# P by V in blocks of four key tiles instead of two, with eight P buffers instead of four

## What is computed

```python
x = x + tanh(g_xattn) * attention(layernorm(x), ctx, ctx, mask, ...)   # 16 batches, 56 queries, 1500 keys, 16 heads of 8
x = x + tanh(g_ffn) * ffn(layernorm(x), ...)                           # 8 experts, top 2, and a shared one
```

```python
q, k, v = query @ qw.T + qb, key @ kw.T + kb, value @ vw.T + vb
scores = einsum('bhqd,bhkd->bhqk', q * DH ** -0.5, k)      # masked to -1e9 where mask == 0
probs = softmax(scores)
out = einsum('bhqk,bhkd->bhqd', probs, v) @ ow.T + ob
```

## Time and profile before

| | |
|---|---|
| time, median of 3 runs | 538.66 us (537.0 to 539.79) |
| the profiled execution | 538.73 us, its span 536.9 us |
| PE busy | 477.6 us, 89% |
| DVE / ACT / POOL busy | 399.8 / 328.4 / 218.7 us |
| 82.20 to 381.30 us (units 1 to 13) | PE busy 296.22 of 299.10 us, DVE 240.87, ACT 200.19, granted clock 1.00, DMA share 0.80 |
| 381.30 to 405.60 us (unit 14) | PE busy 22.26 of 24.30 us |
| 405.60 to 421.30 us (unit 15) | PE busy 14.55 of 15.70 us, ACT 12.27 |
| the spread L307 in step 8 of one unit | starts 285.00, next matmul 285.38 |
| two tiles in unit 15, starts | L363 x16 409.92, L382 x32 410.81, L363 x16 411.71 |

### The profile page before, as it was taken

How to read it: one execution, slowest core, us unless ns; L and a number is a source line. 1 busy time by engine, 2 the same in 40 slices (tenths; PEclk the granted TensorE clock), 3 DMA queues, 4 the chain that set the end, 5 groups by cost and what they waited for, 6 DMA issues and landing times.

```text
span 536.9 us, 15752 instructions
## 1 busy us (share of the span) xinstructions
PE 477.6 (89%) x6779; PEld 355.0 (66%) x6779; DVE 399.8 (74%) x749; ACT 328.4 (61%) x414; POOL 218.7 (41%) x184
## 2 busy tenths in 40 slices
PE   0447699999999999999999999999899867999993
PEld 0114376777768677787777768677688645777772
DVE  6339578787788778888787788778776778766656
ACT  2311367667666666767667666766657737787871
POOL 4034326062351615426062351614645899940000
PEclk9859799999999999999999999999999977999997
DMA  5899976996968869697797968858002121100001
GB/s 161 178 231 199 246 186 143 246 196 172 195 159 189 178 164 190 172 207 138 168 198 173 193 158 190 171 102 188 5 3 80 42 77 43 40 1 2 2 1 35
DMA packets 39806, 72.83 MB, mean 136 GB/s; under 512 B 4638, under 2 KB 26271, under 8 KB 39736
## 3 DMA queue, kind: packets, MB, share of 16 engines
q1 hardware_dynamic: 38456, 70.90, 59.1%
q10 hardware_dynamic: 1280, 0.92, 0.7%
HBM read 24.28 MB, written 0.46 MB: 46 GB/s over the span
## 4 chain that ended last, share of the span: by engine, by line
PE 76%; DVE 8%; DMA 5%; ACT 4%; issue 3%; SPq 2%; POOL 1%; ACTq 0%; DVEq 0%
PE ring L342 16%; PE pv L382 16%; PE st L363 11%; PE ring L324 8%; PE st L828 7%; PE ring L286 7%; PE ring L881 6%; DMA ctxT<-in_ctx 4%; DVE max_part L536 2%; SPq L268 2%; DMA ident_h<-in_c_ident_h 2%; ACT v_ext L469 2%; PE pv L881 2%; PE ring L307 1%; PE ring L350 1%
## 5 line engine op out<-in xcount | busy, mean ns | idle before, releaser
L536 DVE TENSOR_REDUCE max_part<-ring 112x1 f32<-112x512 f32 (+1 forms) x384 | 244.8, 675 | 73.1 <-PE ring L342 73.1
L489 ACT ACTIVATE probs<-st 128x896 f32<-128x896 f32 x192 | 172.6, 916 | 73.5 <-PE st L363 71.3
L342 PE MATMUL ring<-keys,qrs 121*112 121x512 f16 (+1 forms) x384 | 149.6, 391 | 6.8 <-DVE max_part L536 3.2
L363 PEld LDWEIGHTS st<-qrs,keys 121*128 121x128 f16 (+1 forms) x1536 | 97.2, 102 | 29.5 <-issue 8.9
L363 PE MATMUL st<-qrs,keys 121*128 121x112 f16 (+1 forms) x1536 | 106.8, 213 | 1.0 <-ACT qrs L478 1.0
L382 PE MATMUL pv<-probs,v_ext 128*32 128x168 f32 (+3 forms) x3072 | 93.6, 262 | 0.1
L382 PEld LDWEIGHTS pv<-probs,v_ext 128*32 128x32 f32 (+1 forms) x3072 | 73.2, 109 | 21.6 <-issue 11.3
L614 POOL TENSOR_TENSOR k_hi<-k_raw,zero 128x512 f16<-128x512 f32 (+1 forms) x45 | 45.9, 1020 | 86.7 <-ACT k_raw L457 86.7
L342 PEld LDWEIGHTS ring<-keys,qrs 121*112 121x112 f16 x384 | 49.9, 130 | 41.6 <-DVE max_part L536 17.5
L856 DVE TENSOR_TENSOR keys<-probs,keys 128x896 f16<-128x896 f32 (+2 forms) x40 | 45.7, 1144 | 26.1 <-ACT keys L849 26.0
L286 PE MATMUL ring<-ctxT,w_qkv 128*128 128x512 f32 (+1 forms) x94 | 52.9, 649 | 12.9 <-DMA ctxT<-in_ctx 12.9
(11 more groups left out here) (116 smaller groups left out, 404.7 us busy)
## 6 DMA issues: line engine op xcount, KB each, us to landing
ctxT<-in_ctx SPq DMA_DIRECT2D x16, 750.0 KB, 6.4
keys<-mask_add SPq DMA_DIRECT2D x32, 375.0 KB
keys<-k_hi SPq DMA_DIRECT2D x32, 375.0 KB, 6.5
keys<-k_lo SPq DMA_DIRECT2D x32, 375.0 KB, 7.7
keys<-mask_add SPq DMA_DIRECT2D x32, 281.2 KB
mask_raw<-in_mask SPq DMA_DIRECT2D x15, 375.0 KB, 3.6
up_w<-in_up_w SPq DMA_DIRECT2D x9, 256.0 KB, 2.7
down_w<-in_down_w SPq DMA_DIRECT2D x9, 256.0 KB, 3.2
```

The source lines that it names most:

```text
L342: nc.tensor.matmul(ring[0:QW, m % 2, 0:width(c)], qrs[0:ROWS, w, p, :, :].rearrange("r h q -> r (h q)"), keys[0:ROWS, w, p, chunk(c)], sta ...
L363: mm = nc.tensor.matmul(st[0:m, j % 2, p // 4, QW * (p % 4):QW * (p % 4 + 1)], keys[0:ROWS, u, p, j * P:j * P + m], qrs[0:ROWS, u, p, :, : ...
L489: nc.scalar.activation(probs[0:m, j % 4, :].rearrange("p (h c) -> p h c", h=2), st[0:m, j % 2, :, 0:HQ // 2], ACT.Exp).then_inc(s["exps_do ...
L536: nc.vector.tensor_reduce(max_part[:, p, c:c + 1], ring[0:QW, m % 2, 0:width(c)], AX.X, ALU.max).then_inc(s["max_read"], 1)
```

## The change

`probs` gets eight buffers (`PB`), and tile j of unit k uses `slot(k, j)`. P by V is issued for four tiles at a time: tiles 8 to 11 of the batch before in step 3, 0 to 3 in step 7, 4 to 7 in step 11, so three blocks of 64 matmuls in a unit; four tiles instead of two remain behind the last unit. The matmuls are the same. `S_ORDER` places the 24 scores anew (24 places as before; (2,4), (3,3), (5,1) and (7,1) are new, (4,3), (5,4), (8,3) and (9,4) gone), and the normalisation moves from step 1 to step 3. The exp's wait for P by V follows the number of buffers.

```diff
+PB = 8
+QUAD = 4
...
-        probs = sb("probs", [P, 4, HQ])
+        probs = sb("probs", [P, PB, HQ])
...
+        def slot(k, j):
+
+            return (KT * k + j) % PB
...
-        S_ORDER = ((0, 0), (0, 1), (1, 0), (1, 1), (1, 4), (2, 0), (2, 1), (3, 1), (3, 4), (4, 1), (4, 2), (4, 3),
-                   (5, 2), (5, 3), (5, 4), (6, 1), (6, 2), (6, 3), (7, 4), (8, 1), (8, 3), (9, 1), (9, 4), (10, 1))
+        S_ORDER = ((0, 0), (0, 1), (1, 0), (1, 1), (1, 4), (2, 0), (2, 1), (2, 4), (3, 1), (3, 3), (3, 4), (4, 1), (4, 2),
+                   (5, 1), (5, 2), (5, 3), (6, 1), (6, 2), (6, 3), (7, 1), (7, 4), (8, 1), (9, 1), (10, 1))
...
-        NORM_STEP, RECIP_STEP = 1, 8
+        NORM_STEP, RECIP_STEP = 3, 8
...
-                                      probs[0:m, j % 4, S * h:S * (h + n)],
+                                      probs[0:m, slot(k, j), S * h:S * (h + n)],
...
-        LAG = 2
-
-        def pe_pv_pair(pe, b, j):
-
-            k, u, t = b
-            if j % 2 and j > LAG and has(k, 0):
-                for i in (j - LAG - 1, j - LAG):
+        LAG = QUAD
+
+        def pe_pv_quad(pe, b, j):
+
+            k, u, t = b
+            if j % QUAD < QUAD - 1:
+                return
+            if j == QUAD - 1 and has(k, -1):
+                for i in range(KT - QUAD, KT):
+                    pe_pv(pe, (k - 1, buf(b, -1), None), i)
+            if j > QUAD and has(k, 0):
+                for i in range(j - 2 * QUAD + 1, j - QUAD + 1):
                     pe_pv(pe, b, i)
-            if j == LAG - 1 and has(k, -1):
-                for i in range(KT - LAG, KT):
-                    pe_pv(pe, (k - 1, buf(b, -1), None), i)
...
-            if j >= 4 or not known(k, 1):
-                act.wait_ge(s["pv_done"], KT * k + j - 3)
-            nc.scalar.activation(probs[0:m, j % 4, :].rearrange("p (h c) -> p h c", h=2),
+            if KT * k + j >= PB:
+                act.wait_ge(s["pv_done"], KT * k + j - PB + 1)
+            nc.scalar.activation(probs[0:m, slot(k, j), :].rearrange("p (h c) -> p h c", h=2),
```

More of the change, by code:

```diff
@@ L444, in pe_unit @@
                 pe_slot(pe, b, j, 3)
-                pe_pv_pair(pe, b, j)
+                pe_pv_quad(pe, b, j)
                 pe_slot(pe, b, j, 4)
```

## The result

The changed kernel takes 547.45 us (median of 4 runs, 547.16 to 548.49), the kernel before 539.22 beside it; the ratio is 1.016 with a 95% interval of 1.0122 to 1.0198. The forecast was 548.2. The profiled execution took 547.43 us, its span 545.6.

A forecast was written before the change was run, and what follows sets the result against it. TensorE, with the largest busy time, was taken as the bound, DMA not. 13 steady units x 0.53 = 6.9, +0.1 (unit 0), +0.4 (unit 14), +2.05 (unit 15) made +9.5 on 538.73: 548.2 us, range 541.5 to 553.

The forecast's parts named there:

- The price of a block: TensorE entering and leaving one P by V block costs 0.26 us beyond its matmuls; three fewer a unit save 0.79.
- A block of 64 in 1.68: Four-tile P by V block on TensorE: 24 ns a matmul plus 0.13 us, the low end; the high end was 2.01.
- Bank waits: In steps 1 to 3, scores wait for a max to free one of two ring banks: 0.33, 0.33 and 0.30 us.
- (5,1): Score in step 5 waits 0.14 us for its bank behind the normalisation, half as long as the old wait.
- V copies: In steps 5 and 6 the second and third V chunks wait for ScalarE's copies, 0.30 us in all.
- group 11: Last transposed score group of a unit waits 0.37 us on TensorE for exp 9 on ScalarE.
- +0.53 a unit: Each of 13 steady units grows by 0.53 us: waits of 1.96 in place of 0.65, less 0.79 for blocks.
- two real waits: In the old unit, a score behind the normalisation and the second V chunk behind ScalarE's copy wait, together 0.65 us.
- The end passed on whole: The last unit's last block comes 2.05 us later and delays everything to the end by as much; bounds 0.5 and 3.5.
- Rival 1: Faster: scores of steps 1 to 3 do not wait for their bank; unit -0.55 us, total 534; chance 0.08.
- Rival 2: No change: bank waits come, ScalarE's exp and V copy waits do not; unit -0.17 us, total 539; chance 0.07.
- Rival 3: Slower still: long blocks run at the pace of the last 64 matmuls; total 554 to 561 us; chance 0.06.

The follow-up runs named there:

- e6_split_blocks: The changed kernel with one score put into the middle of two of its three P by V blocks a unit; 556.1 us (one run).
- the blocks of three: The changed kernel with P by V blocks of three tiles, scores placed anew, normalisation in step 2, pairs in the last unit; 543.2 us, ratio 1.0089.
- the pairs placed anew: The kernel before, with its blocks of two tiles and four P buffers, and only the score places changed; 533.16 us, ratio 0.9901.
- the fours placed anew: The changed kernel with its blocks of four, score places of its own, normalisation in step 6, pairs in the last unit; 538.84 us, ratio 1.0013.
- e2_old_places: The changed kernel with the score places of the kernel before, normalisation still in step 3; 555.6 us (one run).
- e4_half_exp: The changed kernel with the exp of half of the columns left out, those columns set to one at the start; 544.9 us (one run).

## Why the prediction was right, step by step

- **The price of a block, 0.26:** right in the main; one more switch in the changed kernel costs 0.23 to 0.25 (`e6_split_blocks`).
- **A block of 64 in 1.68:** 1.68. The lower bound was the one to take.
- **Bank waits of 0.33 at (1,4) and (2,4), 0.30 at (3,3):** 0.33, 0.33 and 0.31; and that the loss hangs on them was shown by halving the max. The nearest row, unit 0 of the kernel before, was the same event.
- **(5,1) 0.14, V copies 0.30 in all, group 11 0.37:** measured 0.17, 0.28 and 0.38. The second K chunk and the any row, prices that the layout did not question, happened to have room in this order; in the blocks of three they had none.
- **+0.53 a unit:** +0.53 (23.53 against 23.00). The reading that two real waits stand in the old unit missed a third: score (0,0) starts 1.16 behind the first K chunk, where the next group starts 0.86 behind the second (266.81 to 267.97, 268.81 to 269.67) (ScalarE's copy of the turned maxima, which (0,0) waits for, runs from 266.91 to 267.82). It is as long after the change (246.29 to 247.46), so it drops out of the difference.
- **Unit 0 +0.1, unit 14 +0.4, unit 15 +2.05:** unit 0 can't be told, as all that lies ahead of unit 1 came out -1.1 in one profile and +0.07 in the other; the others +0.44 and +2.08.
- **The end passed on whole:** the size is not settled. Between the up matmul and the end another 0.5 came on top in the profiles of the changed kernel, less than that stretch differs by between kernels with the same work in it, and of 1.3 given back in unit 15 some 0.7 were lost again.
- **The sum, +9.5, 548.2:** +8.7 between the two profiles and +8.2 between the medians (547.45 and 539.22). The units and their waits are right by mechanism; that the total stands within 1 us of the forecast is in part luck, since the early start of that profile (-1.1) and the longer end (+0.5) were not foreseen, and the median of the kernel before was 0.56 higher beside the changed one than the 538.66 that the sum started from.
- **Rival 1 (no bank waits):** its unit was put at -0.55, 22.45; with the max halved it was 22.73, since V copies and the exp then wait in their place (two waits behind one). **Rival 2 (ScalarE's waits do not come):** they came, 0.38 at group 11 and 0.28 at the V chunks. **Rival 3 (slow long block):** 1.68 rules it out.

The two pages of the Trainium skill that were held against the layout both bear on the case. TensorEngine Tiling, Key Properties, says that a change of tiling mode drains TensorE. The trace agrees in that going into a block and out of it costs 0.26 us; that this is a drain, and not another cost of the 128x32 matmuls, no run separates. The step from fp16 to fp32 alone does not cost it: a score ahead of an fp32 V half takes its usual 0.22 (256.44 to 256.66). Perfetto Trace Analysis, Identifying Performance Opportunities, says that a gap that repeats on the engine that should be full can mean too little buffer space. In the steady units of the changed kernel three gaps of 0.31 to 0.33 repeat, each released by a max that had to free one of two banks; the earlier trace rows, which the prediction gives for it, shows such a gap once. In this case a new order shortened the unit from 23.00 to 22.53 with the same two banks.

## What to carry to other kernels

A block that is in the way of one engine may be the cover of another. Before fusing blocks, list what stood between two users of the same two-buffer resource, and see whether something as long as the reader's cycle (here 0.61 us a max) still stands there. When an order is written by hand, lay out one period with start-to-start prices from the trace, all waits included: it told the sign and the size here, and its two large misses (threes) were waits that had been left off the list, not wrong prices.

## What the runs showed of the hardware that was not expected

TensorE now and then stops without a releaser that the profile knows ("issue"). The marked stops in the matmuls of units 0 to 13 last 0.31 to 1.77 us: three in the threes, two in the pairs placed anew, four in the fours placed anew, two in `e2_old_places`, one in `e4_half_exp`, none in the profiles of the other kernels. Ten of the twelve stand inside a block of P by V, two in the turn of the maxima; in the threes all three come 9 or 10 matmuls ahead of the end of the third block of the unit. The kernel before shows one long unit of 23.16 among 13; the version in threes has three (1.1, 2.2 and 0.9 us too long), the pairs placed anew two (0.9 and 0.75), the fours placed anew three (0.6, 1.5 and 0.5). In the stretch 262.5 to 266.5 of the threes, around the longest stop, the instruction queue moved one packet, and other transfers kept the 16 DMA engines 69% busy. That does not mark the stop out: in 217 to 221 of the same profile, where none falls, it also moved one packet, beside 56%, and around the stop of 0.99 us at 287.62 in the fours placed anew the other transfers took 6%. So crowded DMA engines do not explain all of these stops. That they are late fetches of instructions is a guess; no run here took the fetch or the transfers away.
